# Attention layer with 16 heads: the sums of values stay in rows of features on their way through memory

## What is computed

```
q, k, v = (norm(x) @ Wq, norm(x) @ Wk, norm(x) @ Wv), in 16 heads of 16
attn = softmax(where(causal, q k^T, -inf) / sqrt(256))
ctx  = attn @ v                      # per head: sum of exp * v, over the sum of exp
x    = x + ctx @ Wo + bo
x    = x + quantised(norm(x)) @ quantised(weight).T + bias
```

## Time and profile before

| | us |
|---|---|
| median of 3 runs | 2115.71 (2114.38 to 2116.37) |
| profiled execution, whole time | 2120.14 |
| its span | 2118.4 |
| PE busy | 2012.2 (95%) |
| DVE busy | 1739.8 (82%) |
| ACT busy | 1365.3 (64%) |
| POOL busy | 783.3 (37%) |

### The profile page before, as it was taken

The page is one execution under the profiler, slowest core; times in us unless marked ns, Lnnn a source line. Parts: engine busy times, 40 slices in busy tenths (PEclk is TensorE's granted clock), DMA queues, the critical chain, the costliest instruction groups (busy, mean ns, idle before and its releaser), DMA issues.

```text
span 2118.4 us, 36179 instructions
## 1 busy us (share of the span) xinstructions
PE 2012.2 (95%) x12037; PEld 792.0 (37%) x12037; DVE 1739.8 (82%) x4442; ACT 1365.3 (64%) x2905; POOL 783.3 (37%) x1099
## 2 busy tenths in 40 slices
PE   6799899999999999999999999999999999999994
PEld 3333333333333444343333344434333343333433
DVE  4797897878988787888888788796898998888875
ACT  5357666766766666667665666676666666777661
POOL 3323324231435454543324556363143443111232
PEclk9899999999999999999999999999999999999997
DMA  4441221313040322312122231221403112030000
GB/s 153 128 103 54 59 74 37 94 46 97 19 101 26 97 64 72 101 42 87 49 62 58 79 87 63 66 87 49 118 4 101 42 44 57 25 92 24 9 31 20
DMA packets 178327, 138.72 MB, mean 65 GB/s; under 512 B 54486, under 2 KB 178140, under 8 KB 178140
## 3 DMA queue, kind: packets, MB, share of 16 engines
q1 hardware_dynamic: 178140, 136.40, 23.3%
HBM read 85.20 MB, written 50.33 MB: 64 GB/s over the span
## 4 chain that ended last, share of the span: by engine, by line
PE 72%; DVE 16%; ACT 3%; issue 3%; SPq 2%; POOL 2%; DMA 2%; POOLq 0%; DVEq 0%; ACTq 0%
PE psum L1397 21%; PE psum L1380 19%; PE psum L1365 16%; PE psum L1463 7%; DVE max_parts L1108 7%; PE psum L1456 5%; DVE psum L1103 3%; ACT probs L911 2%; PE psum L1432 1%; SPq L633 1%; PE psum L1415 1%; ACT acc_sb L918 1%; PE psum L1485 1%; DMA out_shop<-ctx_scratch 1%; DVE max_parts L1103 1%
## 5 line engine op out<-in xcount | busy, mean ns | idle before, releaser
L911 ACT ACTIVATE probs<-psum 128x512 f32<-128x512 f32 (+3 forms) x2560 | 1213.3, 537 | 527.4 <-PE psum L1380 521.8
L1108 DVE TENSOR_REDUCE max_parts<-psum 128x1 f32<-128x512 f32 x1536 | 968.3, 683 | 130.0 <-PE psum L1365 125.6
L1380 PE MATMUL psum<-q_rows,k_rows 99*128 99x512 bf16 (+3 forms) x2560 | 857.4, 351 | 3.4 <-ACT probs L911 1.6
L1365 PE MATMUL psum<-k_rows,q_rows 96*128 96x512 bf16 (+3 forms) x2560 | 816.6, 350 | 25.8 <-DVE max_parts L1108 10.2
L1397 PE MATMUL psum<-probs,v_in 128*17 128x512 f32 (+3 forms) x5120 | 595.4, 537 | 10.6 <-ACT acc_sb L918 9.9
L1103 DVE CUSTOM_DVE_ANT_0 psum<-psum,causal 128x128 f32<-128x128 f32 (+3 forms) x1024 | 475.9, 519 | 133.4 <-PE psum L1365 130.2
L1380 PEld LDWEIGHTS psum<-q_rows,k_rows 99*128 99x128 bf16 x2560 | 237.2, 97 | 632.0 <-ACT probs L911 496.3
L748 POOL TENSOR_SCALAR_AFFINE_SELECT probs<-probs 128x512 f32<-128x512 f32 x256 | 165.2, 645 | 788.7 <-ACT probs L911 788.3
L1365 PEld LDWEIGHTS psum<-k_rows,q_rows 96*128 96x128 bf16 x2560 | 245.1, 98 | 277.8 <-DVE max_parts L1108 65.3
L1397 PEld LDWEIGHTS psum<-probs,v_in 128*17 128x17 f32 x5120 | 85.8, 95 | 226.9 <-issue 165.0
L1103 DVE DVE_READ_ACCUMULATOR2_ANT max_parts<- 128x1 f32 x1024 | 145.0, 142 | 0.0
(11 more groups left out here) (158 smaller groups left out, 1374.7 us busy)
## 6 DMA issues: line engine op xcount, KB each, us to landing
q_rows<-qk_scratch SPq DMA_DIRECT2D x384, 64.0 KB, 2.6
k_rows<-qk_scratch SPq DMA_DIRECT2D x384, 64.0 KB, 2.7
qk_scratch<-shop SPq DMA_DIRECT2D x56, 384.0 KB, 2.9
shop<-in_L_attn_x SPq DMA_DIRECT2D x19, 512.0 KB, 4.0
v_scratch<-shop SPq DMA_DIRECT2D x16, 544.0 KB, 4.0
v_in<-v_scratch SPq DMA_DIRECT2D x64, 136.0 KB, 2.6
ctx_scratch<-ctx_out SPq DMA_DIRECT2D x60, 128.0 KB, 1.7
out_shop<-in_L_attn_x SPq DMA_DIRECT2D x12, 512.0 KB, 5.4
```

The source lines that it names most:

```text
L911: nc.scalar.activation(probs[s % NPROBS][:, h, a:CHUNK], bank[SCORE_BANKS[n % 3]][:, a:CHUNK], ACT.Exp, scale=SCALE).then_inc(probs_ready, 1)
L1108: nc.vector.tensor_reduce(max_parts[k % 2][:, first:first + heads, t % TILES, c], ring_bank(UNIT_USE[n])[:, 0:heads * width] .rearrange("p ...
L1365: ins = nc.tensor.matmul(dst[:, i * width:(i + 1) * width], q_rows[u][0:ROWS, qc, first + i, t % TILES * P:(t % TILES + 1) * P], k_rows[u] ...
L1380: nc.tensor.matmul(bank[SCORE_BANKS[n % 3]][:, a:CHUNK], k_rows[u][0:ROWS + LEVELS, h, kb * P:(kb + 1) * P], q_rows[u][0:ROWS + LEVELS, qc ...
```

## The change

The copied sums go to memory as they are: 128 rows, of which 68 count, x 512 queries (256 KB where it was 128 KB), straight from `acc_sb`, of which there are now two. The transposes `turn_acc`, the 64 pairs of DVE operations `normalise`, the transposes `turn_ctx` and their 32 ACT copies are gone. For a chunk's output SP loads, for each of four groups of heads, the 64 feature rows into `ctx_in`, laid out as features x tokens, and the 4 rows of denominators, each repeated on its head's 16 rows, into `outT`: 8 DMAs of 64 rows x 512. DVE then takes the reciprocal of `outT`, half by half (128 rows x 2 x 256), POOL multiplies `ctx_in` by it (`weigh`; DVE does it for the last four chunks, `quick_weigh`), and `attend` uses `ctx_in` as it stands. The last four chunks now go through memory too, with a DMA of their own for their last part (`load_last`). The next load into a buffer set waits for the `feed` of the chunk before in this set, where it waited for its `turn_ctx`.

```diff
-    p = by_items(p, 0.45, "turn_ctx")
+    p = by_vector(p, 0.65, "invert")
+    p = by_vector(p, 0.7, "quick_weigh") if quick else by_pool(after(p), 1.3, "weigh")
     p = by_items(p + 1 + (p < TAIL), 1.95, "attend")
...
-    done_at = FIRSTS[k] + SIZES[k] + 1
-    TURNED[k] = item(done_at + 1, 0.45, "turn_acc", k)
-    spend("vector", TURNED[k] + 1, 0.7)
-    if k < NK - QC:
-        sync(TURNED[k] + 2, "store_ctx", k)
+    STORED[k] = FIRSTS[k] + SIZES[k] + 2
+    sync(STORED[k], "store_ctx", k)
...
-            load = max(TURNED[k - QC] + 4, NS - GROUP_STEPS + 2 if before is None else READ_AT[before] + 2)
-            ready = max(TURNED[k] + 1, load + 2)
+            load = max(STORED[k - QC] + 2, NS - GROUP_STEPS + 2, free)
+            last = max(STORED[k] + 1, load)
+            sync(last, "load_last", n)
+            ready = last + 2
         else:
-            load = max(TURNED[k] + 4, free)
+            load = max(STORED[k] + 2, free)
             ready = load + 2
...
             def store_ctx(k):
                 g, qc = divmod(k, QC)
-                sp.wait_ge(vector_emptied, ITEM_NO["turn_acc", k])
...
+                sp.wait_ge(acc_copied, k + 1)
+                sp.dma_start(ctx_scratch[g // QC, qc, g % QC], acc_sb[k % 2][:, :]).then_inc(ctx_stored[k % 2], 16)
+
+            def load_group(n, g):
+
+                w = out_set(n)
+                b, c = divmod(n, QC)
+                k = (QC * b + g) * QC + c
+                sp.wait_ge(ctx_stored[k % 2], 16 * (k // 2 + 1))
+                rows = ctx_scratch[b, c, g].rearrange("(h r) n -> h r n", r=32)
+                to = slice(g % 2 * HG * D, (g % 2 + 1) * HG * D)
+                for t, part in ((ctx_in[w], rows[:, 0:D, :]),
+                                (outT[w], rows[:, D:D + 1, :].broadcast_to([HG, D, CHUNK]))):
+                    sp.dma_start(t[to, g // 2, :], part).then_inc(ctx_loaded[w], 16)
...
                 if before is not None:
-                    sp.wait_ge(for_scalar, ITEM_NO["turn_ctx", before, 1])
+                    sp.wait_ge(for_vector, ITEM_NO["feed", before, 1])
...
+            def weigh(n, a):
+                w = out_set(n)
+                pool.wait_ge(den_inverted, 2 * n + a + 1)
+                mine = half_tokens(ctx_in[w], a)
+                nc.gpsimd.tensor_tensor(out=mine, in0=mine, in1=half_tokens(outT[w], a), op=ALU.mult
+                                        ).then_inc(ctx_ready, 1)
...
             def copy_acc(k):
                 act.wait_ge(values_done, FIRSTS[k] + SIZES[k])
-                if k:
-                    act.wait_ge(for_vector, ITEM_NO["turn_acc", k - 1])
-                nc.scalar.copy(acc_sb[:, :], acc_bank).then_inc(acc_copied, 1)
+                wait(act, ctx_stored[k % 2], 16 * (k // 2))
+                nc.scalar.copy(acc_sb[k % 2][:, :], acc_bank).then_inc(acc_copied, 1)
...
+            def invert(n, a):
+                w = out_set(n)
+                before, times = before_in_set(n)
+                mine = half_tokens(outT[w], a)
+                dve.wait_ge(ctx_loaded[w], 16 * 2 * H // HG * (times + 1))
+                nc.vector.reciprocal(mine, mine).then_inc(den_inverted, 1)
...
             def attend(n, a):
-                pe.wait_ge(scalar_emptied, ITEM_NO["turn_ctx", n, a])
+                pe.wait_ge(ctx_ready, 2 * n + a + 1)
...
-                linear(use, (2 * a, 2 * a + 1), outT[out_set(n)], w_o, False).then_inc(for_vector, 1)
+                linear(use, (2 * a, 2 * a + 1), ctx_in[out_set(n)], w_o, False).then_inc(for_vector, 1)
```

More of the change, by code:

```diff
@@ L295, in before_in_set @@
     return (same[-1] if same else None), len(same)
-TURNED = {}
+STORED = {}
 for k in range(NK):
@@ L330 @@
         if late(n):
-            load = max(TURNED[k - QC] + 4, NS - GROUP_STEPS + 2 if before is None else READ_AT[before] + 2)
-            ready = max(TURNED[k] + 1, load + 2)
+            load = max(STORED[k - QC] + 2, NS - GROUP_STEPS + 2, free)
+            last = max(STORED[k] + 1, load)
+            sync(last, "load_last", n)
+            ready = last + 2
         else:
-            load = max(TURNED[k] + 4, free)
+            load = max(STORED[k] + 2, free)
             ready = load + 2
         sync(load, "load_ctx", n)
[L337 to L340, removed]
+        sync(load, "load_again", n)
+        DONE_AT[n] = [place_output(n, a, ready) for a in range(2)][-1]
 for g in range(NG):
@@ L434, in layer_kernel @@
         probs = [sbuf(f"probs{u}", [HG, CHUNK]) for u in range(NPROBS)]
-        acc_sb = sbuf("acc_sb", [CHUNK])
+        acc_sb = [sbuf(f"acc_sb{u}", [CHUNK]) for u in range(2)]
         max_parts = [sbuf(f"max_parts{u}", [HG, TILES, QC]) for u in range(2)]
@@ L675, in load_ctx @@
                         sp.wait_ge(v_stored[u], 16 * NCH // 2)
[L676 to L679, removed]
+                for g in range(H // HG - late(n)):
+                    load_group(n, g)
             def load_again(n):
@@ L716, in _ @@
                     load_again(n)
+                for n, in at("load_last", p):
+                    load_group(n, H // HG - 1)
             for w in range(NSETS):
@@ L876, in _ @@
                     split_low(r)
+                for n, a in at("weigh", p):
+                    weigh(n, a)
                 for n, a in at("deviation2", p):
@@ L1152, in take_items @@
             def take_items(p):
-                for k, in at("turn_acc", p):
-                    normalise(k)
                 for nothing in at("turn_weights", p):
@@ L1306, in output_work @@
             def output_work(p):
+                for n, a in at("invert", p):
+                    invert(n, a)
+                for n, a in at("quick_weigh", p):
+                    quick_weigh(n, a)
                 for n, a in at("stats2", p):
@@ L1434, in turn_half @@
                 ins.then_inc(for_scalar, 1)
-            def turn_ctx(n, a):
-                w = out_set(n)
-                loads = sum(ctx_groups(m) for m in range(n + 1) if out_set(m) == w)
-                pe.wait_ge(ctx_loaded[w], 16 * loads)
-                if late(n):
-                    pe.wait_ge(vector_emptied, ITEM_NO["turn_acc", NK - NCH + n])
-                turn_half(ITEM_USE["turn_ctx", n, a], ctx_in[w], a)
-            def turn_xd(n, a):
-                pe.wait_ge(xd_ready, 2 * n + a + 1)
-                turn_half(ITEM_USE["turn_xd", n, a], grid[out_set(n)].rearrange("p (j e) -> p j e", j=TILES), a)
             def project(n, m):
```

81 lines of the change are left out of this document (20 added, 61 removed).

## The result

| | before | after |
|---|---|---|
| median of the runs | 2116.04 us (2114.38 to 2121.48, 4 runs) | 2302.51 us (2300.80 to 2309.02, 4 runs) |
| profiled execution, span | 2118.4 us | 2299.1 us |
| last score matmul starts at | 2066.6 us | 2230.7 us |
| from there to the end of the span | 51.8 us | 68.4 us |

A forecast was written before the change was run, and what follows sets the result against it. PE's instruction stream was taken to bound the kernel. -44 + 58 + 8 + 11 = +33 us on 2115.7 gave 2149 us; low and high ends +7 and +70 (2123 to 2186), range with the rivals 2076 to 2194.

The forecast's parts named there:

- loads and their use: SP issuing eight loads for four: 1.3 us more, half counted for each of 12 chunks, +8 us (0 to 16).
- reciprocals in the steps: Long DVE reciprocals, 3.1 us each, hold up PE's units: 4.5 us a pair, 13 chunks, +58 us.
- PE, and what else is gone: Transposes and some waits leave PE: -44 us (38 to 48); work removed from DVE and ACT gives no time.
- the end: Behind the last unit: chunks 13 and 14 on DVE +10, later attend +2, chunk 15 -1; +11 us (9 to 14).
- at reciprocals for loads: Sign of a wrong forecast: PE waiting mostly there would put the cost into the way through memory, not the reciprocal.
- The flat reading: Rival on DVE's reciprocal: surcharge per instruction, 0.77 us for 512 elements; 2082 us in all; chance 0.23.
- the second reading: DVE's reciprocal works element by element, 5.9 ns each plus 0.158 us, 3.2 us for 512; 3.1 taken; chance 0.58.
- The clock: Rival: PE's clock falls behind its waits, 13 x 1.5 = 20 us, 2169 us; chance 0.09, shared with a dearer reciprocal.

The follow-up runs named there:

- e10_full_div: Changed kernel, complete with its reciprocals, loads reordered to a slowest dimension of 16 and work planned six steps behind its loads, not two: 2164.76 us, ratio 1.021.
- e5_patient: Changed kernel with loads reordered to a slowest dimension of 16, reciprocals replaced by a product with 1.0, work planned six steps behind loads, not two: 2092.49 us.
- e2_sixteen: Changed kernel, complete, with its loads' rows in the order (feature, head), so the slowest dimension is 16, not 4; w_o loaded likewise: 2222.51 us, ratio 1.050.
- e7_fewer: Kernel before the change, with three of the four transposes of a piece left out in turn_acc: 2110.42 us, ratio 0.996.
- e6_dense: Changed kernel with 16-way loads; denominators loaded once as 128 x 64, inverted, stored, then loaded repeated; loading starts about four steps before weighing: 2107.92 us, ratio 0.9945.
- e8_end_early: Dense-denominator kernel e6_dense with the last chunk's work planned at once behind its loads, not two slots later, and less room for invert_last: 2102.96 us, ratio 0.992.
- e4_own_rows: Changed kernel with the denominators' load reading 64 different rows instead of 4 rows 16 times each; size and order unchanged: 2300.94 us.

## Why the prediction failed, by its own steps

The runs give the whole difference of the profiled executions as a sum. Loads: after minus e10_full_div. Reciprocals: e10_full_div minus e5_patient. The remainder is e5_patient against before. The last score matmul starts at 2230.7, 2094.4, 2023.0 and 2066.6 us in these, and what follows it lasts 68.4, 68.5, 68.3 and 51.8 us.

| term | forecast | measured |
|---|---|---|
| loads and their use | +8 (0 to 16) | **+136** |
| reciprocals in the steps | +58 (42 to 85) | +72 |
| PE, and what else is gone | -44 (38 to 48) | -44 |
| the end | +11 (9 to 14) | +17 |
| sum | +33 | +181 |

**The loads are the step that failed,** put at +8 us (0 to 16) and measured at +136. Two readings in it were wrong.

The first is the landing. The prediction priced what SP pays to issue the loads, 1.3 us more a chunk, and took the landing from the earlier trace rows, where a load went from 128 rows of memory to 128 rows (the 2.5 us there are of stores and loads together; the loads alone have 3.0). The new load has another shape, heads first, and I put no landing time of its own on it. The needed question was: how many engines carry it? The rule of the Trainium skill told above, from "DMA: Bandwidth & Descriptors", answers it, and was missed; an estimate by it, a quarter of the engines, would have made 2.5 us of landing into some 10 a load.

The second is the overlap: "the first use is still two steps, 6.2 us, behind the first issue". At five chunks DVE stood there within 2.6 us of the first issue, because SP's program has its row loads in front, and so nearly every microsecond until the landing became a wait, on 16 engines too. The text did name the wait ("at reciprocals for loads"), under what would prove it wrong, but gave it no mechanism and no price.

Of the 136 us about 80 go with the engines (after to e2_sixteen, 85 in the step part: 2230.7 to 2145.8) and the rest with the use. In the other order it is 106 us for the later use alone (2230.7 to 2125.0, eight steps) and 31 us for the engines (to 2094.4, with six steps): the two overlap, since a slow load costs only what its user waits.

**The reciprocals: right in kind, and near in size for a reason that was only half right.** The flat reading, 0.77 us, is refuted: 544 ns for 64 numbers, 1720 for 256 and 3346 for 512 lie within 25 ns of one line, 6.25 ns a number and 0.14 us fixed, as the second reading had it (5.9 and 0.158). PE's two waits at the first chunk of e10_full_div add to 4.28 us, the forecast's 4.5. But over all chunks its waits grew by 37 us, not by 58; the clock, which the sum put at nothing, made up 28. That the sum of this term is near is in part luck. The three differences of medians with and without division (71.2, 71.5, 72.3 us) set this against a cheap instruction, not against nothing. They are 86% of the 83 us by which DVE's busy time differs (1801.9 against 1719.0). The reciprocals of chunks 13 and 14, which I had put at the end, stand before the last score matmul and so in the steps. Without the price of the loads, e10_full_div is 46 us slower than before: the sign came out for the forecast's reason too.

**PE's term: the right sum, partly by luck.** The steps gave 43.6 us, but e7_fewer shows that transposes by themselves return 9 of 21. The change also takes 43 us of DVE's work and 32 copies of ACT's, which I valued at nothing because "neither engine sets the steady part". With DVE at 84% that was too simple. How much each contributes was not measured.

**The end: right sign, wrong mechanism.** I had given it to the reciprocals. But it lasts 68.5 us with them and 68.3 without. The longer way and the later places of chunks 14 and 15 are what is left as a cause of the 16.6 us; no run separates them. It is longer still with the dense denominators, 78.1 us in e6_dense and 76.4 in e8_end_early. In e6_dense the last loads were issued at 2036 us and used at 2063.5, because the plan puts them behind the end of chunk 14 on DVE.

**The range's upper end** was added up wrongly: by the stated bounds it is -38 + 85 + 16 + 14 = +77, where the text has -41 and 12 in it and +70. The measured time lies beyond either.

**The clock** was a rival at +20 us. Its mean granted value over the span tells its extent (before 0.985, in this order after, e10_full_div, e5_patient):

```profile
core 0: 2299.1 us, clock 0.939
```
```profile
core 0: 2162.9 us, clock 0.968
```
```profile
core 0: 2091.3 us, clock 0.980
```

With levels 0.5 and 1, that is 280 us at the lower level in after (2 x 0.061 x 2299), 138 and 84 us in the other two, and 64 in before. The same 11653 instructions were busy 2019.7, 2002.8 and 1974.9 us. So of the 136 us some 17 lie in longer busy time, and of the 72 us 28, more than the rival's 20. The clock amplified the stalls and was hardly a cause of its own, since it nearly goes when they go.

## What to carry to other kernels

For every DMA whose shape a change alters, write down the slowest dimension of both sides before anything else; four heads in front cost 80 us here. A plan that places the use of a load must know two times: how long this shape takes to land, and when the issuing engine really comes to it, since two steps in the plan were none in time. One number in the plan (108 us here) loses what the change gains. Invert a number before it is repeated, not after. A stall of PE costs twice: the wait, and the lower clock behind it.

## What the runs showed of the hardware

- A load of 64 rows x 2 KB with a slowest dimension of 4 leaves five completion events; eight of them had landed 18.7 us behind the first issue at chunk 0, and a 512 KB load behind such eight took 14.0 us. With 16 in front each leaves sixteen events and lands in 2.9 us, the one behind in 5.1.
- SP's issues slow down behind such loads: at chunk 0 the twelve row loads took 7.1 us in front of them (496.4 to 503.5) and 9.3 us behind (510.1 to 519.4).
- Reading one row of memory 16 times is as fast as reading 16 rows (e4_own_rows, 2300.9 against 2302.5 us).
- A reciprocal on DVE costs 6.25 ns for each number of a row (64 numbers 544 ns, 512 numbers 3346 ns), six times a product's 1.04 ns.
- PE's stall of 20.7 us was followed by matmuls at the lower clock, 1.2 GHz (523 to 530 us: granted 0.50); the one at 535.3 us took 0.39 us, as at 2.4 GHz, where those at 526.7 took 0.61.
